# Line sweeps of a four-layer network: which engine adds the first stage's result

## What is computed

```python
x = x + _L0_conv_ref(_gn(x), ...)      # a state-space scan and a 3x3 convolution
x = x + _L1_conv_ref(_gn(x), w_down, w_up, w_right, w_left)
x = x + _L2_conv_ref(_gn(x), ...)
x = x + _L3_conv_ref(_gn(x), ...)      # a deformable convolution

# layer 1, one direction of four:
def step(prev, cur):
    new = cur + jax.nn.relu(_conv1d(prev, w))      # 9 taps, 128 x 128 channels
    return (new, new)
```

## Time and profile before

| | before |
|---|---|
| three runs, us | 7547.92, 7555.20, 7561.26 |
| the profiled execution's own time, us | 7543.92 |
| its span from first to last instruction, us | 7542.1 |
| mean granted TensorE clock | 0.908 |
| VectorE busy in the span | 5448.8 us, 72% |
| GpSimd busy in the span | 4360.4 us, 58% |
| layer 1, from its first instruction to the last statistics | about 2192.7 to 3950.7 us |

### The profile page before, as it was taken

One profiled execution on the slowest core, in us unless ns is written; L12 is line 12 of the kernel. 1 busy time (PEld: TensorE's weight loads), 2 busy tenths in 40 slices (PEclk: granted clock), 3 DMA queues, 4 the chain that ended last, 5 costly groups with the idle time before them and its releaser, 6 DMA issues. The chain is left out here.

```text
span 7542.1 us, 100137 instructions
## 1 busy us (share of the span) xinstructions
PE 6254.1 (83%) x20845; PEld 3314.4 (44%) x20845; DVE 5448.8 (72%) x12602; ACT 3408.7 (45%) x6458; POOL 4360.4 (58%) x4002
## 2 busy tenths in 40 slices
PE   4999999999969999999958777777778777776653
PEld 2444444444448888888843222222222222222221
DVE  5999999999975555666672577767677676776667
ACT  4777777777741111222212344444444444444444
POOL 4999999999930000100020577777777777777774
PEclk9999999999989999999979999888898888887655
DMA  4444444444440000000013577767677677777767
GB/s 180 169 178 177 168 169 169 168 167 168 169 159 0 3 0 0 0 0 0 0 59 89 159 210 219 213 208 209 207 213 214 204 209 213 207 217 215 207 198 280
DMA packets 418136, 1130.86 MB, mean 150 GB/s; under 512 B 61476, under 2 KB 193906, under 8 KB 376306
## 3 DMA queue, kind: packets, MB, share of 16 engines
q0 software_dynamic: 187200, 629.56, 28.4%
q1 hardware_dynamic: 230456, 496.79, 18.9%
HBM read 997.65 MB, written 128.46 MB: 149 GB/s over the span
## 5 line engine op out<-in xcount | busy, mean ns | idle before, releaser
L1202 POOL DMA_INDIRECT d_ring<-corner_table,d_idx_now x2304 | 2387.5, 1036 | 822.5 <-issue 448.4
L1522 DVE SCALAR_TENSOR_TENSOR d_mix<-d_ring,d_w_now,d_mix 128x128 f32<-128x128 f32 x6912 | 1945.1, 346 | 870.2 <-ACT d_mix L1265 845.5
L1265 ACT ACTIVATE d_mix<-d_ring,d_w_now 128x128 f32<-128x128 f32 x2304 | 909.8, 400 | 1663.1 <-DMA d_ring<-corner_table,d_idx_now 1567.0
L936 POOL TENSOR_TENSOR X<-X 128x512 f32<-128x512 f32 x1024 | 1289.3, 1276 | 182.2 <-DVE X L974 176.4
L1367 PE MATMUL d_ps_s<-small,d_mix 128*128 128x128 f32 x2304 | 626.3, 348 | 828.6 <-DVE d_mix L1522 826.0
L274 PE MATMUL prop_ps<-prop_parts,prop_w_hi 128*128 128x512 f32 x4536 | 1178.5, 404 | 1.3 <-DVE prop_parts L282 1.3
L974 DVE TENSOR_TENSOR_SCAN X<-X,m_pB 128x512 f32<-128x512 f32 x896 | 1132.9, 1270 | 0.0
L843 PE MATMUL m_pY<-X,small 128*128 128x512 f32 x2048 | 1030.7, 600 | 31.2 <-POOL X L936 28.5
L1367 PEld LDWEIGHTS d_ps_s<-small,d_mix 128*128 128x128 f32 x2304 | 336.9, 152 | 1474.9 <-DVE d_mix L1522 1215.4
L274 PEld LDWEIGHTS prop_ps<-prop_parts,prop_w_hi 128*128 128x128 f32 x4536 | 820.8, 189 | 189.5 <-DVE prop_parts L282 1.5
L242 ACT ACTIVATE prop_parts<-X 128x256 fp32r (+1 forms) x512 | 276.6, 541 | 1383.5 <-DVE X L298 1383.0
(11 more groups left out here) (224 smaller groups left out, 7038.5 us busy)
## 6 DMA issues: line engine op xcount, KB each, us to landing
X<-c_scratch SPq DMA_DIRECT2D x256, 1024.0 KB, 4.9
corner_table<-d_tT SPq DMA_DIRECT2D x512, 128.0 KB
d_ring<-corner_table,d_idx_now POOLq DMA_INDIRECT x2304, 3.7
X<-in_x SPq DMA_DIRECT2D x8, 2048.0 KB, 23.3
m_res<-in_x SPq DMA_DIRECT2D x64, 256.0 KB, 4.7
x_scratch<-m_res SPq DMA_DIRECT2D x64, 256.0 KB, 2.0
X<-x_scratch SPq DMA_DIRECT2D x8, 2048.0 KB, 9.5
prop_x<-x_scratch SPq DMA_DIRECT2D x8, 2048.0 KB, 11.7
```

Source lines behind the costliest of these rows:

```text
L936: pool.tensor_tensor(hc[:, n % NHC, :], h[:, n, :], Cb[:, n, :], ALU.mult).then_inc(s.HC, 1)
L1202: pool.indirect_dma_start(out=ring[:, m % RING, :], out_offset=None, in_=flat, in_offset=bass.IndirectOffsetOnAxis(ap=idx_now[:, m:m + 1], ...
L1265: act.activation(R[:, k % 3, t, :], ring[:, m % RING, 0:P], ACT.Copy, scale=w_now[:, par, 4 * m:4 * m + 1]).then_inc(s_r0, 1)
L1522: dve.scalar_tensor_tensor(R[:, k % 3, t + j, :], ring[:, m % RING, corner * P:(corner + 1) * P], w_now[:, par, 4 * m + corner:4 * m + cor ...
```

## The change

```diff
     NG, NI, PAD, LINES = 2, 4, TAPS // 2, H - 1
     NB = 3
-    ON_POOL = (1, 2, 4, 5, 7)
+    ON_POOL = ()
```

## The result

The changed kernel takes 7522.73 us (median of six runs, 7515.18 to 7532.12), the kernel before, with three more runs, 7556.21. The ratio is 0.9956, with a 95% interval of 0.9943 to 0.9969: 33.5 us faster, where 6.5 were forecast and 7541 to 7557 was the range. The profiled execution took 7521.81 us (span 7520.0) against 7543.92 (7542.1), so 22.1 us are there to be found between the two traces.

What follows compares the result with a forecast made beforehand. VectorE alone was taken to bound layer 1's end: 28.8 us of stalls go, 22.3 us of additions come, loads and the stage behind count nothing, so 7555.2 - 6.5 = 7548.7 us; range 7541 to 7557.

Steps and rivals of the forecast that it cites:

- What bounded the end of layer 1: At layer 1's end VectorE alone is the path, without a gap from 3868.12 to 3951.21 us.
- the stalls: At layer 1's end, four VectorE instructions held by GpSimd's additions return to usual length: 28.8 us go.
- the additions: Five images' additions move from GpSimd onto VectorE's chain at layer 1's end, 4.46 us each: 22.3 us come.
- the schedule: Layer 1's end summed instruction by instruction: next layer's scales start at 3944.7 us instead of 3951.21, 6.5 us gained.
- four coinciding ends: At layer 1's end, four long VectorE instructions end where a GpSimd addition ends plus their usual time, within 0.2 us.
- 16 statistics in 9.00 us: Rows cited to claim loads don't slow statistics: 9.00 us at 434 GB/s, 9.64 us for 16 with none.
- GpSimd's additions were free: Rival at layer 1's end: the long instructions have another cause and stay, 7577.5 us; chance 0.03.
- the loads become the limit: Rival at layer 1's end: loads landing after over 23.2 us make VectorE wait, 7552 us at 25; chance 0.03.
- Nothing arrives at the end: Rival: the stage after layer 1 swallows the 6.5 us gain, leaving 7555 us; chance 0.05.
- The stage behind: After layer 1's end: starts 6.5 us earlier, code moves some ten instructions; effect taken as nothing, 5 us either way.
- a better course by 9 us or more: Rival: the stage after layer 1 happens to run better beside the gain, 7540 us or less; chance 0.03.
- theory 1: From follow-ups: before, the last stage's image loop top ends an 8192-byte VectorE code piece, so each jump waits twice.

Runs made afterwards that it cites:

- b_late: Kernel before, GpSimd's additions kept but held until both groups' sweeps are through; one run, 8212.4 us on a slow chip, layer 1's end 72.70 us.
- the pair: Kernel before and changed kernel, both with the last stage's image and chunk-pair loops written out: 7479.3 and 7470.4 us on one chip.
- b_dve6: Kernel before, GpSimd's additions kept, six VectorE semaphore counts added after layer 1's last statistics, moving code by five in effect: 7523.2 us, ratio 0.9977 to before.
- a_dve125: Changed kernel with 123 more VectorE instructions where VectorE is otherwise idle, 128 with the change's five: 7538.3 us, ratio 0.9998 to the kernel before.
- a_chunkloop: Changed kernel with only the last stage's loops over chunk pairs written out, image loop kept: 7540.9 us, ratio 0.9980 to the kernel before.
- a_unroll3: Changed kernel with the last stage's loops over images and chunk pairs both written out: 7470.4 us, ratio 0.9892 to the kernel before.
- a_dve123: Changed kernel with 121 more VectorE instructions in an otherwise idle block, code 126 from its place before: 8209.6 us on a slow chip, ratio 0.9992 to before.
- b_dve5: Kernel before, GpSimd's additions kept, five VectorE semaphore counts added, moving code by four in effect: 8193.6 us on a slow chip, ratio 0.9974 to before.

## Why the prediction failed

*What bounded the end of layer 1, the stalls, the additions.* Right, term by term. Stalls of 28.8 us went, five additions of 4.46 came; 6.67 us measured, 6.47 in the schedule. An addition beside a load takes 4.41 us, the lower bound that was taken. What the prediction calls the fixed part of an instruction shows in three sizes: 128x512, 128x2048 and 128x4096 took VectorE 0.69 (line 1411), 2.29 and 4.42 us in the kernel before, which is 0.16 us and 1.04 ns for each of the 512, 2048 or 4096. The loads, one at a time now, landed after 7.0 to 7.5 us. b_late showed the cause of the long instructions, which until then was only read off from four coinciding ends. Two readings were looser than they sound, and nothing came of it. "16 statistics in 9.00 us" under traffic counts two that the stretch cuts off; at the usual 0.594 us 15.2 fit into 9.00 us, so the traffic made no difference. And GpSimd worked beside the first 24 statistics for their last 1.8 us only, from 3902.74.

*The rivals.* "GpSimd's additions were free" fell with the first timeline; "the loads become the limit" too. "Nothing arrives at the end" fell: with loops written out the pair is 8.9 us apart.

*The stage behind.* This step failed. It named the code that moves ("some ten instructions"; the traces have five more on VectorE and 14 fewer on GpSimd), said that no row prices it, took nothing, and gave 5 us either way; a better course by 9 us or more had a chance of 0.03, and "only the spread of the runs" for it. In its place the runs showed a gain of 16.9 us from the place of VectorE's code alone (b_dve6), and a loss of 16.8 from its return (a_dve125, the cost of its own instructions taken off). There was a row for it in the trace of before, which the prediction doesn't read: four times a gap of 6.2 us "issue" ahead of line 1406, right behind the jump. With the records of VectorE's sequencer it would have said that 11 us of second gaps stand behind the loop's first instruction, out of 25 us in all, and may hang on where five instructions push the loop's top. By theory 1, which only the later runs showed, five more push it over the edge of a piece, to the faster side; the range would have had to reach down to some 7520 (an estimate: 7548.7 less 25 and less some of the 5 us that it allowed).

*Does it cost what it lasts?* The four second waits last 11.3 us and cost the path 15.7 us by the starts of the gathers and about 17 us by the medians (16.9 and 16.8). Why the path pays more than the wait isn't settled. In the trace of before GpSimd's gathers go on through both gaps of the second jump, while TensorE's next weight load has waited 10.7 us for VectorE and ScalarE's next instruction 16.2 us; no run takes this apart. The first waits seem to be worth less than they last where they were removed (10 of some 25 us at the chunk loop, counted across two kernels that differ in other waits too).

*What stays open* is also how the recorded 33.5 us are made up: 6.7 at layer 1's end and about 17 by the place of the code make 24. The second measurement of the change, 23.3 us, agrees with that; the first has an interval of 23 to 43 us, so that 24 lies at its edge, and the other 10 us are chance or something that no run showed. The 70 us between a_chunkloop and a_unroll3 are more than all of VectorE's waits after the image loop's jumps (27.7 us): waits against constants in place of registers and the other engines' jumps are in it, and weren't taken apart.

*What a jump costs.* VectorE's first wait behind the image loop's jump took 2.7 to 3.7 us in the kernel before and 3.0 to 3.5 in the changed one, each with a packet of q14 in it. The packets of q14 are of 8192 bytes, and the place of the second wait repeats after 128 instructions (a_dve125). The other queue, q8, has 71 packets of 16384 bytes in both kernels; by the count in a_unroll3 (256.2 instructions a packet) it carries TensorE's code.

## What to carry to other kernels

Before giving VectorE's work to GpSimd (or taking it back), look at what VectorE does at that moment: here an addition of GpSimd held VectorE's instructions with both operands in SBUF until it was done (8.59, 8.25, 11.25 and 10.93 us where 0.76, 0.61, 4.42 and 4.42 are usual), an addition of VectorE held GpSimd's in the same way (13.01 us where 8.80 is usual), eight statistics took 4.85 us beside one as without, and by the traces starting GpSimd's part one step later shortened the end of the layer more (72.7 us) than taking it away (76.4 us). And when an edit adds or removes even a few instructions ahead of a loop with a long body, look for "issue" time behind the loop's jumps: it moves with the code, by 0.2% here, and it can pass for the edit's own effect. A copy of the old kernel with as many idle instructions put in tells the two apart, if one reads from its trace what these cost by themselves: 123 of them cost 4.7 us here.

## What had not been expected of the hardware

- A jump back in the last stage's loops costs VectorE 2.7 to 4.1 us before the first instruction (2.4 to 3.0 us at the last of the jumps over chunk pairs). Another 2.2 to 3.9 us came ahead of the second, third or fourth instruction, by where the code stands in steps of 128 instructions (8192 bytes): by this count where the loop's first one (before, a_dve125), two (a_chunkloop) or three (a_dve123) instructions are the last of a piece. With 124 (the changed kernel, b_dve6) or 125 (b_dve5) left in the piece there was no second wait.
- 123 semaphore instructions in a row took VectorE 11.7 us (3949.1 to 3960.8), 0.095 us each, though each is recorded with 0.021 us.
- Of two additions of 128x4096 float32, one on each engine and with both operands in SBUF, the one that started 0.17 us later waited for the other: 12.93 us on GpSimd, where 8.80 is usual.
- The kernel before took 7540, 7556 and 7558 us and, on two other chips, 8215 and 8221 us. The stages ahead of the last took the same time on all of these to 4.2 us, in the traces of all the kernels here (the last start of line 298 at 3866.97 to 3871.18 us).
